# Key tiles of 128 in the first loop: five tiles of 108 become four of 128 and one of 8 that serves four heads at once

## What is computed

```python
def _L1_attn_ref(x, sc_token, W_qkv, W_proj, b_proj):
    ...
    xt = jnp.concatenate([x, jnp.broadcast_to(sc_token, (B,) + sc_token.shape[1:])], axis=1)
    qkv = (xt @ W_qkv).reshape(B, N1, 3, H, Dh)
    ...
    attn = jax.nn.softmax(jnp.einsum('bhqd,bhkd->bhqk', q, k) * scale, axis=-1)
    out = jnp.einsum('bhqk,bhkd->bhqd', attn, v)
    ...
    return out @ W_proj + b_proj
```

## Time and profile before

| what | before |
| --- | --- |
| median of 3 runs | 1954.89 us (1948.09 to 1955.36) |
| the profiled execution | 1950.34 us, its span 1948.7 us |
| TensorE busy | 1802.1 us (92%), 11904 instructions |
| VectorE busy | 1245.7 us (64%), 3509 |
| ScalarE busy | 1064.6 us (55%), 2547 |
| POOL busy | 287.6 us (15%), 441 |
| exponentials (L967) | 1536, mean 439 ns |
| score products (L1379) | 1536, mean 312 ns |
| value products (L1394), instructions | 3072, mean 450 ns |

### The profile page before, as it was taken

The page is one execution under the profiler, slowest core; times in us unless marked ns, Lnnn a source line. Parts: engine busy times, 40 slices in busy tenths (PEclk is TensorE's granted clock), DMA queues, the critical chain, the costliest instruction groups (busy, mean ns, idle before and its releaser), DMA issues. The chain is left out here.

```text
span 1948.7 us, 41468 instructions
## 1 busy us (share of the span) xinstructions
PE 1802.1 (92%) x11904; PEld 1240.9 (64%) x11904; DVE 1245.7 (64%) x3509; ACT 1064.6 (55%) x2547; POOL 287.6 (15%) x441
## 2 busy tenths in 40 slices
PE   5799999999999999999999987779999999999996
PEld 4566677667667667667677654346666666666664
DVE  3356766776766767777777675347776566665653
ACT  1245555565555555555555554346656566666662
POOL 5211120120110211111111111010110000100010
PEclk9889999999999999999999999899999999999998
DMA  4212212221221231221221223123343333343331
GB/s 165 61 33 53 78 57 56 67 69 49 66 79 40 62 84 35 70 78 35 70 78 42 57 77 86 38 75 94 88 116 97 86 99 97 91 112 95 96 89 29
DMA packets 161304, 143.62 MB, mean 74 GB/s; under 512 B 32284, under 2 KB 136488, under 8 KB 161064
## 3 DMA queue, kind: packets, MB, share of 16 engines
q1 hardware_dynamic: 157448, 136.69, 26.3%
q0 software_dynamic: 2304, 4.79, 1.0%
q10 hardware_dynamic: 1440, 0.75, 0.1%
HBM read 82.79 MB, written 50.16 MB: 68 GB/s over the span
## 5 line engine op out<-in xcount | busy, mean ns | idle before, releaser
L967 ACT ACTIVATE prob<-sps 108x324 f32<-108x324 f32 x1536 | 616.3, 439 | 371.3 <-PE sps L1379 358.7
L1237 DVE TENSOR_REDUCE mxh<-mps 108x1 f32<-108x324 f32 x1152 | 515.0, 486 | 279.0 <-PE mps L1413 277.1
L1379 PE MATMUL sps<-qpack,kpack 128*108 128x324 bf16 x1536 | 418.7, 312 | 23.9 <-ACT prob L967 6.8
L1413 PE MATMUL mps<-kpack,qpack 96*108 96x324 bf16 x1728 | 384.6, 292 | 16.8 <-DMA kpack<-scr_k 6.2
L1413 PEld LDWEIGHTS mps<-kpack,qpack 96*108 96x108 bf16 x1728 | 211.5, 129 | 140.4 <-issue 41.2
L1379 PEld LDWEIGHTS sps<-qpack,kpack 128*108 128x108 bf16 x1536 | 186.0, 127 | 168.1 <-ACT prob L967 100.0
L1394 PE MATMUL aps<-prob,v 128*32 128x324 f32 x3072 | 290.0, 450 | 2.6 <-DVE gmall L1225 1.1
L1365 PE MATMUL lin<-yT,w 128*128 128x324 f32 x576 | 182.6, 448 | 12.5 <-ACT g L867 9.6
L1237 DVE TENSOR_REDUCE mxs<-mps 108x2 f32<-108x392 f32 x288 | 160.6, 558 | 17.3 <-PE mps L1413 13.6
L1365 PEld LDWEIGHTS lin<-yT,w 128*128 128x128 f32 x576 | 101.5, 190 | 58.3 <-issue 27.4
L783 POOL CAST piece<-rest 128x324 bf16<-128x324 f32 x96 | 43.5, 453 | 638.7 <-DVE rest L1068 634.8
(11 more groups left out here) (150 smaller groups left out, 2308.6 us busy)
## 6 DMA issues: line engine op xcount, KB each, us to landing
qpack<-scr_q SPq DMA_DIRECT2D x96, 243.0 KB, 3.2
kpack<-scr_k SPq DMA_DIRECT2D x96, 121.5 KB, 3.3
scr_q<-piece SPq DMA_DIRECT2D x32, 243.0 KB, 3.0
scr_k<-piece SPq DMA_DIRECT2D x32, 243.0 KB, 3.6
kpack<-scr_k SPq DMA_DIRECT2D x96, 81.0 KB, 3.1
bc<-rec_d SPq DMA_DIRECT2D x112, 60.8 KB, 2.4
scr_q<-piece SPq DMA_DIRECT2D x32, 162.0 KB, 3.3
scr_q<-piece SPq DMA_DIRECT2D x64, 81.0 KB, 2.9
```

The source lines that it names most:

```text
L967: nc.scalar.activation(prob[0:rows, n % NP, :], sps[0:rows, n % 2, 0:N], ACT.Exp, scale=SCALE).then_inc(att.exped.sem, 1)
L1237: nc.vector.tensor_reduce(dst, src, AX.X, ALU.max, negate=True).then_inc(att.mps.free["dve"].sem, 1)
L1379: mm(sps[0:rows, n % 2, 0:N], kpack[:, 4 * q + n % 4, k * att.rows:k * att.rows + rows], qpack[:, 4 * q + n % 4, :], start=True, stop=True ...
L1413: done = mm(bank[0:P, s * SC:s * SC + k1 - k0], qpack[0:6 * D, 4 * q + hd, t * P:(t + 1) * P], kpack[0:6 * D, 4 * q + hd, k0:k1], start=Tr ...
```

## The change

- The first loop's tiles are 128 keys (`TK1`), so tiles 0 to 3 hold 512 keys and the last one 8. Tile 2 holds the last 68 own keys and the first 60 shared ones.
- The scores of the last tile are one unit for four heads: four products of 32 columns (8 keys and 24 columns of zeros) into the partitions 0, 32, 64, 96 of one bank, then one exponential of 128 partitions, then one value product with `v1s`, which holds the four heads' values of the 8 keys in a 128 by 128 block. A group has 17 units in place of 20, a pass 51 in place of 60.
- These units have slots of `prob` of their own (`NP + GROUPS`); `Attention.prob` gives the slot of each unit and the wait for it.
- As 51 is odd, the first unit of a pass waits for the last exponential of the pass before.
- The second loop has values of its own (`v2`). Setup has seven more memsets.
- `ORDER_1` is another table. `ORDER_2` differs in the places of `p` alone. The ratio in `woven` is another.

```diff
-TK1, KT1 = P, 5
+TK1, KT1 = 128, 5
...
+NK1P = (KT1 - 1) * TK1 + 32
...
 ORDER_1 = (
-    "ln2_1 a m",
-    "s v_0.0 shared s m s v_0.1 m s m",
...
+    "a v_0.0 m s s ln2_1 shared m v_0.1",
     "m s m",
...
+        self.single = 4 * (kt - 1) if halves == 2 else None
-        self.units = H * kt
+        self.per = 4 * kt if halves == 1 else 4 * kt - 3
+        self.units = GROUPS * self.per
...
+    def prob(self, n):
+
+        q, r = divmod(n, self.per)
+        if r == self.single:
+            return NP + q, n + 1 - self.units
+        v = n - q * (self.single is not None) - NP
+        return v % NP, v + 1 + (v // self.single if self.single else 0)
...
-        kpack = sb("kpack", [KP, H, NK1], bf16)
-        v1 = sb("v1", [KP, KT1, H, 32])
+        kpack = sb("kpack", [KP, H, NK1P], bf16)
+        v1 = sb("v1", [KP, KT1 - 1, H, 32])
+        v1s = sb("v1s", [128, GROUPS, 4, 32])
+        v2 = sb("v2", [KP, KT2, H, 32])
...
-        prob = sb("prob", [128, NP, N])
+        prob = sb("prob", [128, NP + GROUPS, N])
...
-                while rest and (0.025 + 1.144 * rest[0][0] / len(two.items)) * len(one.items) <= n and not held(rest[0][1]):
+                while rest and (-0.023 + 1.156 * rest[0][0] / len(two.items)) * len(one.items) <= n and not held(rest[0][1]):
...
             def quad(att, i, n):
...
-                pe.wait_ge(att.exped.sem, att.exped.at(i, n - 1))
-                mm(sps[0:rows, n % 2, 0:N], kpack[:, 4 * q + n % 4, k * att.rows:k * att.rows + rows],
-                   qpack[:, 4 * q + n % 4, :], start=True, stop=True).then_inc(att.scored.sem, 1)
+                pe.wait_ge(att.exped.sem, att.exped.at(i, n - 1 if n or att.units % 2 == 0 else 0))
+                if r == att.single:
+                    for hd in range(4):
+                        done = mm(sps[32 * hd:32 * hd + 32, n % 2, 0:N], kpack[:, 4 * q + hd, k * att.rows:NK1P],
+                                  qpack[:, 4 * q + hd, :], start=True, stop=True)
+                    done.then_inc(att.scored.sem, 1)
+                    return
...
             def sums(att, j, i, slot):
...
+                n0 = att.per * q + 4 * k
+                if 4 * k == att.single:
+                    pe.wait_ge(att.exped.sem, att.exped.at(j, n0 + 1))
+                    mm(aps[:, 0:N], v1s[:, q].rearrange("p h d -> p (h d)"), prob[:, att.prob(n0)[0], :],
+                       start=False, stop=True).then_inc(att.summed.sem, 1)
+                    return
```

More of the change, by code:

```diff
@@ L393, in build @@
         one = Attention("own_shared", KT1, TK1, 2, v1, ORDER_1, OFF_1, lin, mps, signal, -2)
-        two = Attention("own", KT2, TK2, 1, v1, ORDER_2, OFF_2, lin, mps, signal, -1)
+        two = Attention("own", KT2, TK2, 1, v2, ORDER_2, OFF_2, lin, mps, signal, -1)
         front, moe = one.lin, two.lin
@@ L539, in build @@
         gate_pe, gate_pool, gate_sp = signal("gate_pe", 0), signal("gate_pool", 0), signal("gate_sp", 0)
[L541 removed]
+        MEMSETS_POOL, SETUP_POOL, SETUP_DVE = 20, 24, 9
         block = ctx.enter_context(nc.Block())
@@ L617, in pack @@
                 sp.sem_inc(gate_sp.sem)
-                sp.wait_ge(att.exped.sem, att.exped.at(j - 1, 4 * att.kt * (q + 1)))
+                sp.wait_ge(att.exped.sem, att.exped.at(j - 1, att.per * (q + 1)))
                 if comes_first(att, j):
-                    sp.wait_ge(one.exped.sem, one.exped.at(B - 1, 4 * KT1 * (q + 1)))
+                    sp.wait_ge(one.exped.sem, one.exped.at(B - 1, one.per * (q + 1)))
                 sp.dma_start(qpack[0:6 * D, 4 * q:4 * q + 4, 0:N],
@@ L742, in _ @@
             REST = ((xS[KC:KP, :, :], 0.0), (v1[:, :, :, :], 0.0), (kpack[KC:KP, :, :], 0.0), (yA[KC:KP, :, :], 0.0),
-                    (v1[:, 0:KT1 - 1, :, D:D + 1], 1.0), (v1[0:LAST1, KT1 - 1, :, D:D + 1], 1.0),
-                    (kpack[6 * D:6 * D + 3, :, :], 1.0), (yA[KC:KC + 1, :, :], 1.0), (bc[:, :, :], 1.0))
+                    (v1[:, :, :, D:D + 1], 1.0), (v1s[:, :, :, :], 0.0), (v2[:, :, :, :], 0.0), (v2[0:P, :, :, D:D + 1], 1.0),
+                    *((v1s[32 * hd:32 * hd + LAST1, :, hd, D:D + 1], 1.0) for hd in range(4)), (kpack[0:KC, :, NK1:NK1P], 0.0),
+                    (kpack[6 * D:6 * D + 3, :, 0:NK1], 1.0), (yA[KC:KC + 1, :, :], 1.0), (bc[:, :, :], 1.0))
             def memsets(sets, done):
@@ L964, in quad @@
                 act.wait_ge(att.scored.sem, att.scored.at(i, n + 1))
-                act.wait_ge(att.summed.sem, att.summed.at(i, n - NP + 1))
-                rows = att.tile[n // 4 % att.kt]
-                nc.scalar.activation(prob[0:rows, n % NP, :], sps[0:rows, n % 2, 0:N], ACT.Exp,
+                slot, summed = att.prob(n)
+                act.wait_ge(att.summed.sem, att.summed.at(i, summed))
+                rows = 128 if n % att.per == att.single else att.tile[n % att.per // 4]
+                nc.scalar.activation(prob[0:rows, slot, :], sps[0:rows, n % 2, 0:N], ACT.Exp,
                                      scale=SCALE).then_inc(att.exped.sem, 1)
@@ L973, in sums @@
                     q = slot // att.kt
-                    act.wait_ge(att.summed.sem, att.summed.at(j, 4 * (slot + 1)))
+                    act.wait_ge(att.summed.sem, att.summed.at(j, att.per * (q + 1)))
                     if q == 0 and att is one:
@@ L1320, in shared_keys @@
                     done.then_inc(setup_pe.sem, 1)
-                for m, p in enumerate((TK1, LAST1)):
+                for k in range(2):
+                    done = mm(sps[0:TK1, 0, 0:C], xS[:, k, (KT1 - 2) * TK1:(KT1 - 1) * TK1], w_qkv[:, k, 2 * C:],
+                              start=k == 0, stop=k == 1)
+                done.then_inc(setup_pe.sem, 1)
+                for hd in range(4):
                     for k in range(2):
-                        done = mm(sps[0:p, m, 0:C], xS[:, k, N + m * TK1:N + m * TK1 + p], w_qkv[:, k, 2 * C:],
+                        done = mm(sps[32 * hd:32 * hd + LAST1, 1, 0:C], xS[:, k, (KT1 - 1) * TK1:NK1], w_qkv[:, k, 2 * C:],
                                   start=k == 0, stop=k == 1)
-                    done.then_inc(setup_pe.sem, 1)
+                done.then_inc(setup_pe.sem, 1)
             def shared_in():
@@ L1369, in quad @@
                 kt = att.kt
-                q, k = divmod(n // 4, kt)
+                q, r = divmod(n, att.per)
+                k, hd = divmod(r, 4)
                 rows = att.tile[k]
@@ L1375, in quad @@
                     pe.wait_ge(one.exped.sem, one.exped.at(B - 1, one.units))
-                if n % (4 * kt) == 0:
+                if r == 0:
                     pe.wait_ge(att.rows_in.sem, att.rows_in.at(i, 16 * (q + 1)))
-                pe.wait_ge(att.exped.sem, att.exped.at(i, n - 1))
-                mm(sps[0:rows, n % 2, 0:N], kpack[:, 4 * q + n % 4, k * att.rows:k * att.rows + rows],
-                   qpack[:, 4 * q + n % 4, :], start=True, stop=True).then_inc(att.scored.sem, 1)
+                pe.wait_ge(att.exped.sem, att.exped.at(i, n - 1 if n or att.units % 2 == 0 else 0))
+                if r == att.single:
+                    for hd in range(4):
+                        done = mm(sps[32 * hd:32 * hd + 32, n % 2, 0:N], kpack[:, 4 * q + hd, k * att.rows:NK1P],
+                                  qpack[:, 4 * q + hd, :], start=True, stop=True)
+                    done.then_inc(att.scored.sem, 1)
+                    return
+                mm(sps[0:rows, n % 2, 0:N], kpack[:, 4 * q + hd, k * att.rows:k * att.rows + rows],
+                   qpack[:, 4 * q + hd, :], start=True, stop=True).then_inc(att.scored.sem, 1)
             def sums(att, j, i, slot):
@@ L1390, in sums @@
                         pe.wait_ge(one.copied.sem, one.copied.at(B - 1, GROUPS))
-                for n in range(4 * slot, 4 * slot + 4):
-                    hd = n % 4
+                n0 = att.per * q + 4 * k
[4 more added lines that the diff above has]
+                    return
+                for hd in range(4):
+                    n = n0 + hd
                     pe.wait_ge(att.exped.sem, att.exped.at(j, n + 1))
-                    mm(aps[32 * hd:32 * hd + 32, 0:N], att.values[:, k, 4 * q + hd, :], prob[:, n % NP, :],
-                       start=k == 0, stop=k == kt - 1).then_inc(att.summed.sem, 1)
+                    mm(aps[32 * hd:32 * hd + 32, 0:N], att.values[:, k, 4 * q + hd, :], prob[:, att.prob(n)[0], :],
+                       start=k == 0, stop=k == kt - 1 and att.single is None).then_inc(att.summed.sem, 1)
             def maxima(att, i, q, n):
@@ L1503, in first_step @@
                     front.emptied(pe, i - 1, "t3_1")
-                    by_token(front, i, what, 2 * k + c, *pair(xS, w_qkv, 2 * C), P, last)
+                    by_token(front, i, what, 2 * k + c, *pair(xS, w_qkv, 2 * C), TK1, last)
                 elif name == "proj4":
```

20 lines of the change are left out of this document (11 added, 9 removed), and 25 rows, old and new, of the table ORDER_1.

## The result

The change makes no difference that matters: 1954.47 us (median, 1950.06 to 1962.51) against 1950.79 for the kernel before, run beside it (1945.04 to 1958.67), a ratio of 1.0022 with a 95% interval of 1.0013 to 1.003. The forecast was 1929 and its range ended at 1945. What came is nearest to rival B's time, 1950. The profiled execution has a span of 1954.2 us, where it was 1948.7.

The account below looks back on a forecast made before the run. TensorE was taken to set the pace: 1.85 us less work a pass, 1.65 arriving, less 0.2 for loads, 1.45; times 15 passes, 22 off 1950.3, so 1928, forecast as 1929 us, range 1909 to 1945.

Parts of the forecast that it names:

- rival B: First-loop passes: the 1.45 us gain meets +0.8 of other waits and +0.54 of switches, leaving 1950 us; chance 0.10.
- steps 1 to 3: TensorE per pass: scores save 1.2 us, values 0.1, fewer tiling switches 0.55; sum 1.85 us less work.
- Rival C: Narrow score groups: four products run one after another, 1.0 us a group instead of 0.16, 1966 us; chance 0.03.
- The 128-column loads: Score weight loads on TensorE: 20 columns more show behind some maxima, 0.2 us a pass, bounds 0 and 0.25.
- rival E: Score weight loads: 128 columns take no longer than 108, 15 x 0.2 us less, 1926 us; chance 0.25.
- Other waits: TensorE's remaining waits in a pass, some 2.2 us: changes net about 0, bounds -0.6 and +0.8.
- 1.65 arrive: Per pass: of 1.85 us saved, 0.2 is waited for again between first query product and next batch's first maximum.
- 0.9 us to spare: Stretch from first query product to next first maximum: `kpack`'s DMA chain still ends last, by 0.9 us.
- rival D: Roots behind `hx` end last: with 0.86 us extra the time stays 1929, slower only from 2.35 on; chance 0.02.
- The turn: Woven stretch of both loops, where TensorE idles 38 us of 200: gain 0, bounds 8 us either way.
- Second loop and setup: Second loop's order: 0, bounds -2 and +2 us; setup's larger memsets, some 2 us, hidden by POOL's idle time: 0.
- the extra switches: Tiling switches on TensorE: without help from neighbours, three more pairs a pass, 0.54 us; taken as 0.

Follow-up runs that it names:

- ln4_early: The change with `ln4_0` and `ln4_1` moved ahead of `out_0.1`, as in the kernel before: 1943.17 us, ratio 0.9959 to the kernel before.
- before_hx: The kernel before with one step moved, `hx` (POOL's sum of two tiles) behind `hc`, some 17 us earlier in the pass: 1947.94 us, ratio 0.9982.
- hx_st: ln4_hx with `ln1_0` moved behind `qk0`: 1939.72 us, ratio 0.9931 to the kernel before.
- old_ratio: The change with the turn rule of the kernel before: 1954.46 us, ratio 1.0029 to the kernel before.
- before_cut: before_hx with two transfers fewer, a measuring probe whose scores lack their smallest term: 1938.22 us, ratio 0.9938 to the kernel before.
- ln4_hx: ln4_early with `hx` moved behind `hc`: 1939.65 us, ratio 0.9948 to the kernel before.
- tiles_old_table: The new tiles with the order tables and turn rule of the kernel before: 1952.22 us, ratio 1.0011 to the kernel before.

## Why the prediction was wrong

**The work (steps 1 to 3) was right.** Less TensorE work, 1.70 us a pass, forecast 1.85. A narrow score group takes 0.15 us before a value group and 0.25 before an `out` product, so the share of the tiling switch is 0.1 as put. Rival C is out: the four narrow products run side by side.

**The 128-column loads cost nothing.** I took +0.2 us a pass. Weight loads of the change by form (busy, mean ns, idle before):

```profile
L1408 PEld LDWEIGHTS sps<-qpack,kpack 128*128 128x128 bf16 x768 | 73.0, 100 | 101.4 <-ACT prob L985 60.7 <-issue 27.7 <-DMA qpack<-mT 2.7
L1408 PEld LDWEIGHTS sps<-qpack,kpack 128*108 128x108 bf16 x576 | 69.8, 128 | 68.7 <-ACT prob L985 45.1 <-issue 15.1 <-DMA qpack<-mT 0.7
```

A load of 128 columns takes 100 ns, less than one of 108 with 128 ns. A score product starts 83 ns after a 196-column maximum in both kernels, where I had 10 to 20 ns more. So rival E's condition is met, and the term of 3 us was 0. The Trainium skill's rule (TensorE: Matmul & The Clock Gate, Weight-path perf modes) is that a faster load comes on by itself at 128 weights that are not fp32. The trace agrees, with these 100 and 128 ns.

**The step that failed is "Other waits ... Net about 0, bounds -0.6 and +0.8".** Measured, waits rose by 1.7 us a pass. The largest is one that I looked for in the wrong place: I put +0.4 on `t4_1`, for `out_1`, and followed only TensorE's distance to it. The wait is 0.86 ahead of `t4_0`, and comes from VectorE's order: the words between `ln4_0` and `ln4_1` had changed, and VectorE reads the same table. Shown by ln4_early, which gives back 0.83 a pass. `t3`, `inv` and `proj` went about as estimated. Another part, the 0.47 us in the value group ahead of `r`, had no term.

**"1.65 arrive" failed too, in its "0.9 us to spare".** The stretch was fixed, as said; it is 15.9 us, forecast 16.1. But it has two chains of nearly equal length. One goes over VectorE and `hx`, which holds up a two-input operation for 0.6 to 1.1 us; I had the row of 1.18 us and used it only for rival D, where I put the excess at 0.86; before_hx shows 0.17 for the operation alone, so it is 1.0 there and 1.1 in the body. The other is `kpack`'s. In the change the issue of the last store to `scr_k` ends 8.47 us after `qk0`, 0.5 later than before. VectorE does `ln1`'s statistics ahead of the first rest and a maximum ahead of the second, and hx_st shows that taking the first away isn't enough. In the body of the change `kpack` lands 0.12 to 0.47 us ahead of the first maximum, and where a maximum of the loop waits for it the figure is 0.12; so the landing leaves an estimated 0 to 0.35, not 0.9, and little that is saved just ahead of or in the stretch can pass it. The waits by name were half right: `t1` waits 1.1 (forecast 1.8), `zv` waits 0.15 (forecast 0.25), and the wait for `mp` ahead of `r` went, as forecast.

**The turn.** I took 0 with bounds of 8; the profiled execution has +6.7, at a lower clock. Of that, old_ratio shows that the turn rule isn't the cause. ln4_early takes 260.7 us there, nearly as before, but before_hx, whose order differs from before's by one word, takes 266.2. One profile of each can't tell the order's part from what varies by itself. But all the runs tell of the clock. Its mean over a run is 0.974 to 0.983 in the 69 runs of the kernel before that the experiments have beside them (0.978 on average), and 0.977 on average in before_hx and in before_cut. In the 20 runs of the change it is 0.965 to 0.975 (0.971), and in the other ten kernels with the new tiles 0.968 to 0.974 on average, whatever their order. Among the change's runs, one with 0.001 less took about 1 us more, so the lower clock goes with an estimated 6 us. That it costs them isn't shown, for waits may lie behind both, and the cause of the 6.7 stays open. Second loop and setup were right at 0: the second loop's `fin` products span 596.7 us, before 597.3.

Rival B came true in its first half alone: waits rose, by twice its bound, and the extra switches didn't come; that its time fits is in part luck. The chance of 0.10 was too small because B was priced as two bounds hit at once. The 5 us of waits in a pass weren't an amount that work can be taken away from; they were where chains of other engines ended.

## What to carry to other kernels

When work is taken from the engine that sets the pace, list the chains of the other engines that end within a microsecond or two of it, and take the gain only where none does; here 1.7 us less work a pass came back as 1.7 us of waits, and moving one layernorm step freed half of it. If a table of order is read by every engine, go through it once for each engine: a word that is harmless for TensorE can put VectorE's next step behind a product. Of the kernels that compute all of it, ln4_hx and its three variants are the fastest and level with each other: 1939 to 1941 us, 0.5 to 0.7% under the kernel before.

## What the runs showed of the hardware

- A VectorE operation with two inputs from memory waits for a running GpSimd operation to end: 0.17 us alone, 0.78 to 1.34 beside `hx` in the loop's body of six kernels, ending within 0.03 us of it in each. The Trainium skill (SBUF — State Buffer, Who interferes with whom) calls it a lock that the later one waits for in full; the traces agree, with these times. In before_hx the scaling of `xn`, one input and a scalar, met `hx` at its new place and took 1.47 us instead of 0.37.
- Behind a wait of 1.76 us in tiles_old_table, the granted clock fell in some passes and not in others of the same order (0.57 and 1.00 over 4 us), at 1.5 us each.
- The bf16 load of 128 columns is faster than that of 108, 100 ns against 128; one of 32 columns takes 94.
